# A four-layer graph kernel: smaller-edge masks of a quarter's own blocks move from VectorE to ScalarE, and one share step moves behind them

## The chip, the cores and the metric

The kernel runs on one core of a Trainium2 chip. The metric is the device time of the whole program in microseconds (us), lower being better. Profiles come from one execution each; times in a profile count from the start of its span. TensorE is written PE, VectorE DVE, ScalarE ACT, GpSimd POOL and the DMA-issuing engine SP.

## What is computed

4096 nodes carry 64 features each. A 4096 x 4096 adjacency (about 1.6% of entries are positive, the diagonal is full, the rest zero) is used by four layers, each followed by a residual sum and a normalization of each row:

```python
x = _layernorm(x + _L0_gnn_ref(x, adj, L0_gnn_weight))      # Chebyshev, three products with adj
x = _layernorm(x + _L1_gnn_ref(x, adj, adj, ...))           # two GRU cells and a signed attention
x = _layernorm(x + _L2_gnn_ref(x, adj, ...))                # last 100 neighbours with decay
x = _layernorm(x + _L3_gnn_ref(x, adj, ...))                # hyperbolic aggregation
```

The change is in the second layer, whose core is

```python
A = adj - diag(diag(adj))
node_support = concat([(A > 0) @ h, (A < 0) @ h])
h_plus, h_minus = (A > 0) @ hw, (A < 0) @ hw
e_plus, e_minus = leaky_relu(concat([h_plus, h_minus]) @ a), leaky_relu(concat([h_minus, h_plus]) @ a)
att = softmax(where(A > 0, e_plus, where(A < 0, e_minus, -9e15)))
edge_support = (att * A) @ hw
```

An attention score depends only on the row and the sign of the edge. So the kernel needs four sums over neighbours of each node: with the positive part of A, with the negative part, with the 0/1 mask of edges above zero and with the 0/1 mask of edges below zero. It forms all four, although this input has no edge below zero.

## The kernel before

The second layer works on four quarters of 1024 columns (`q`, 0 to 3). Each quarter streams all 4096 rows through a ring of three slots of SBUF as 16 pairs (`m`, 0 to 15) of row blocks, a pair being 128 partitions x 2048 float32. For each pair:

- ACT makes `negs` = relu(-edges) (L1684), then on even pairs `less` = sign(negs) (L1688), then the codes that the third layer reads (`make_codes1`, L1665), and issues the store of these codes.
- DVE takes two steps of a running count of edges (`extend_chain`, L2405), makes `more` = edges > 0 (L2411), on odd pairs `less` = edges < 0 (L2441), and turns the edges into max(edges, 0) in place (L2444, called the rectified edges here), which must wait for `negs`.
- PE multiplies the rectified edges and `negs` (`edge_products`, L1088 and L1089; called the edge block here) and the two masks (`mask_products`, L1104; the mask block). On even pairs the edge block comes first, on odd pairs the mask block.

In a quarter's **own pairs**, those with m // 4 == q, the columns and rows meet on the diagonal. There DVE does more: it reads the diagonal (L2423, L2427) and cuts it out of the edges (L2430), between and behind its two chain steps. Only then may ACT read the edges (it waits for `diag_cut`), and DVE make the masks. On the other pairs ACT need not wait for DVE.

Orders are written out by hand, and each engine runs its own in sequence; semaphores tie them. Three of these ties matter below. The second chain step of pair m waits until ACT has made the codes of pair m - 1 (`extend_chain`: `codes_made`), so its room can be written again. `negs` and the masks have room for two pairs, so making those of pair m waits until PE is through with pair m - 2 (`pair_used`). And `mask_products` waits for all masks of the pair before its first matmul.

Work of the quarter before is spread over the pairs of the present one: `score_gate` (DVE, after m = 3), `exps` (ACT, m = 4), `share_gate` (DVE, after m = 5: small steps and the copy L2304), `spread_shares` (PE, before the products of m = 7, L1017), `weigh_sums` (DVE, after m = 8, L2310), `hidden` (PE, m = 11 and 12; it needs `weigh_sums`), `read_hidden` (ACT), and from the third quarter on the transposes and products of the third layer (`turn_rows`, `copy_rows`, `supports`). In the last quarter ACT also makes the first decays of the third layer (L1651) at m = 14 and 15, and `new_state` (L1589) at m = 15.

Of the kernel before, what the change touches and what calls it, by code (L numbers as in the profile page):

```python
# [7 lines left out]
ALU = mybir.AluOpType  # L8
# [38 lines left out]
def adjacency_stack(nc, adjT, x, xT, cheb_w, gatWT, gat_a2, wieT, wheT, bie, bhe, winT, whnT, bin_, bhn,  # L47
# [5 lines left out]
    with ctx:  # L53
# [11 lines left out]
        with ExitStack() as under:  # L65
            under.enter_context(nc.sbuf_tensor("ring_low", [P, RING1, GB, QC], F32))
            less = under.enter_context(nc.sbuf_tensor("less", [P, 2, 2, QC], F32R))
# [245 lines left out]
        n = 0  # L313
        for quad, end in enumerate(quad_ends):
            late = quad >= len(quad_ends) - 2
            n = max(n, end + (2 if late else 3), LAST_AT + 4)
# [25 lines left out]
            return u if u and u.turned else None  # L342

        PAIRS = 2 * NS
        L2_TILES = [(Q, s) for part in ((1, 2, 3, 0), (4, 5), (6, 7)) for Q in (0, 1) for s in part]
        L2_TILES += [(Q, s) for Q in (2, 3) for s in range(NS)]

# [93 lines left out]
        less_made = sem("less_made")  # L441
        masks_made = sem("masks_made")
# [197 lines left out]
        def used1(T):  # L640

            return 2 + 2 * (T + 1)

        def later_after(chain, j):

# [204 lines left out]
        def _(pe):  # L850
# [241 lines left out]
            def mask_products(q, m, r):  # L1092

                pe.wait_ge(masks_made, q * PAIRS + m + 1)
                if m % 2 == 0:
                    pe.wait_ge(less_made, (q * PAIRS + m) // 2 + 1)
                for i in range(2):
                    start, stop = m == 0 and i == 0, m == PAIRS - 1 and i == 1
                    for t, masks in enumerate((more, less)):
                        if start and q:  # L1100
                            pe.wait_ge(sums_copied[0], 3 * q - 1 + t)
                        for h in range(2):
                            cols = slice(h * HALF, (h + 1) * HALF)
                            mm = nc.tensor.matmul(ps[:, 2 + 2 * t + h, :], parts[:, 2 * m + i, :],  # L1104
                                                  masks[:, m % 2, i, cols], start=start, stop=stop)
                return mm

            for q in range(NQ):
                for m in range(PAIRS):
                    s, pair = divmod(m, 2)  # L1110
                    r = slot1(q, s)
                    if q == 0 and m == 10:
                        pe.wait_ge(turn_read, turns0)
                        turn_row_sums(NB - CB, NB, 7, visits[-1])
                    if q and m == 0:
                        turn_h(q - 1)
                    if q and m == 2:
                        score(q - 1)
                    if q and m == 7:
                        spread_shares(q - 1)  # L1120
                    if q >= 2 and m == 9:
                        turn_rows(q - 2)
                    if q >= 2 and m == 10:
                        supports(q - 2)
                    if q == 0 and m % 4 == 0:
                        pe.wait_ge(rest_made[0][0], s // 2 + 1)
                    hides = q and m in (11, 12)
                    if hides:
                        hidden(q - 1, 2 * (m - 11))
                    if m % 2:  # L1130
                        mask_products(q, m, r)
                        if hides:
                            hidden(q - 1, 2 * (m - 11) + 1)
                        edge_products(q, m, r).then_inc(pair_used, 1)
                    else:
                        edge_products(q, m, r)
                        if hides:
                            hidden(q - 1, 2 * (m - 11) + 1)
                        mask_products(q, m, r).then_inc(pair_used, 1)
# [308 lines left out]
        def _(act):  # L1448
# [76 lines left out]
            for a in visits:  # L1525
# [4 lines left out]
                if a.t in COUNT_TURN_AT:  # L1530
                    m = COUNT_TURN_AT.index(a.t)
# [139 lines left out]
            for q in range(NQ):  # L1671
                for m in range(PAIRS):
                    s, pair = divmod(m, 2)
                    r = slot1(q, s)
                    if q == 0 and m == 7:
                        norm_act(act, NQ - 1)
                        act.preload_act_table_set("exp_and_others")
                    if q == 0 and m == 9:
                        split_act(act, NQ - 1)
                    act.wait_ge(loaded[r], loads(q, s))  # L1680
                    if s // 2 == q:
                        act.wait_ge(diag_cut, m + 1)
                    act.wait_ge(pair_used, q * PAIRS + m + 1)
                    nc.scalar.activation(negs[:, pair], ring[:, r, 2 * pair:2 * pair + 2, :], ACT.Relu,  # L1684
                                         scale=-1.0).then_inc(negs_made, 1)
                    if m % 2 == 0:
                        act.wait_ge(negs_made, q * PAIRS + m + 1)
                        nc.scalar.activation(less[:, pair], negs[:, pair], ACT.Sign).then_inc(less_made, 1)  # L1688
                    make_codes1(q, m)
                    if q and m == 0:  # L1690
                        copy_sums(q - 1)
                    if q and m == 1:
                        copy_h(q - 1)
                    if q and m == 4:
                        exps(q - 1)
                    if q >= 2 and m == 7:
                        root1(q - 2)
                    if q >= 2 and m == 9:
                        copy_rows(q - 2)
                    if q >= 2 and m == 10:  # L1700
                        read_supports(q - 2)
                        part2(q - 2, 0)
                    if q and m == 11:
                        read_hidden(q - 1, range(2))
                    if q and m == 12:
                        read_hidden(q - 1, range(2, 6))
                    if q and m == 13:
                        read_hidden(q - 1, range(6, CB))
                    if q >= 2 and m == 13:
                        part2(q - 2, 1)  # L1710
                    if q and m == 15:
                        new_state(q - 1)
                    if q >= 2 and m == 15:
                        part2(q - 2, 2)
                    if q == NQ - 1 and m in (14, 15):
                        make_decays(m - 14)
# [230 lines left out]
        def _(dve):  # L1947
            V = nc.vector
# [459 lines left out]
            def make_more(q, m, edges):  # L2408

                dve.wait_ge(pair_used, q * PAIRS + m + 1)  # L2410
                return V.tensor_scalar(more[:, m % 2], edges, 0.0, None, ALU.is_gt)  # L2411

            for q in range(NQ):
                for m in range(PAIRS):
# [3 lines left out]
                    edges = ring[:, r, 2 * pair:2 * pair + 2, :]  # L2418
                    if m == 0:
                        open_chain(q)  # L2420
                    if s // 2 == q:
                        mine = own_blocks(ring[:, r], s % 2, pair)
                        V.tensor_tensor(own, mine, ident[:].unsqueeze(1).broadcast_to([P, 2, P]),  # L2423
                                        ALU.mult).then_inc(diag_steps, 1)
                        extend_chain(q, 2 * m, edges[:, 0, HALF:QC])
                        dve.wait_ge(diag_steps, 2 * m + 1)
                        V.tensor_reduce(diag[:, 2 * m:2 * m + 2], own, AX_X, ALU.add).then_inc(diag_steps, 1)  # L2427
                        extend_chain(q, 2 * m + 1, edges[:, 1, HALF:QC])
                        dve.wait_ge(later_made, later_after(NQ + q, min(2 * m + 2, NB - 1)))
                        V.tensor_tensor(mine, mine, offdiag[:].unsqueeze(1).broadcast_to([P, 2, P]),  # L2430
                                        ALU.mult).then_inc(diag_cut, 1)
                        dve.wait_ge(diag_cut, m + 1)
                    else:
                        extend_chain(q, 2 * m, edges[:, 0, HALF:QC])
                        if m % 2:
                            make_more(q, m, edges)
                        extend_chain(q, 2 * m + 1, edges[:, 1, HALF:QC])
                    if m % 2:
                        if s // 2 == q:
                            make_more(q, m, edges)  # L2440
                        V.tensor_scalar(less[:, pair], edges, 0.0, None, ALU.is_lt).then_inc(masks_made, 1)  # L2441
                    dve.wait_ge(later_made, later_after(NQ + q, min(2 * m + 2, NB - 1)))
                    dve.wait_ge(negs_made, q * PAIRS + m + 1)
                    V.tensor_scalar(edges, edges, 0.0, None, ALU.max).then_inc(rect_ready, 1)  # L2444
# [26 lines left out]
                        score_gate(q - 1)  # L2471
                    if q >= 2 and m == 4:
                        centre_rows(1, q - 2)
                    if q and m == 5:
                        share_gate(q - 1)
                    if q >= 2 and m == 6:
                        row_spread(1, q - 2)
                    if q >= 2 and m == 7:
                        scale_rows1(q - 2)
                    if q and m == 8:  # L2480
                        weigh_sums(q - 1)
                    if m == PAIRS - 1:
                        cut_own_edges(q)
# [495 lines left out]
```

## Time and profile before

| | us |
|---|---|
| median of 3 runs | 1470.06 |
| lowest and highest run | 1464.03, 1471.13 |
| the profiled execution | 1466.39 |
| its span, first to last instruction | 1464.7 |
| second layer in its trace, about | 477 to 907 |

Over the span PE is busy 90%, DVE 82%, ACT 67%, POOL 15%. A busy PE is not one at its peak: the page models the ends of matmuls. The page has a row of the clock granted to TensorE; in this kernel it is 2.4 GHz nearly throughout, and falls to 1.2 GHz in short stretches. A timeline row gives the start, the duration, the engine, the line, the operands and their shape, and in brackets how long the engine was idle before and what released it. The difference to the metric (1.7 us here) lies outside the span.

### The profile page before, as it was taken

The numbers are of one execution on the slowest core, as the hardware profiler recorded it, in microseconds if no ns is written. First come the engines' busy times: TensorE is split into PE (matmuls) and PEld (weight loads), VectorE is DVE, ScalarE is ACT, GpSimd is POOL, SyncE is SP. The second block draws the span as 40 slices with busy tenths as digits, with TensorE's granted clock in tenths as the row PEclk, the third lists the DMA queues.
The fourth block names the chain that finished last, engine by engine and source line by source line (L and its number), as shares of the span: only waits on it lengthen the run. The fifth ranks groups of instructions, "written<-read, shape, count | busy, mean of one in ns | idle before, by whom it ended". The sixth has DMA issues, their size and how long they took to land. (4 is left out here: it accounts for less than half of the span.)

```text
span 1464.7 us, 18440 instructions
## 1 busy us (share of the span) xinstructions
PE 1322.8 (90%) x6874; PEld 589.6 (40%) x6874; DVE 1201.0 (82%) x1554; ACT 983.7 (67%) x919; POOL 222.6 (15%) x150
## 2 busy tenths in 40 slices
PE   6899999999898999999999999989978888888893
PEld 1233334334334444444544554544423433334342
DVE  5898978995887888867977977558688898899997
ACT  0001444894583677567677767786789899999985
POOL 1000000000000000000000001152133354444450
PEclk9999999999998999999999999999889999999995
DMA  9999979998999555544535532244534666546610
GB/s 360 409 409 409 372 263 413 409 391 325 415 409 413 199 200 197 191 150 173 194 134 190 191 136 103 75 150 147 203 114 126 202 172 216 193 153 222 218 50 29
DMA packets 134561, 341.56 MB, mean 233 GB/s; under 512 B 7877, under 2 KB 57481, under 8 KB 134281
## 3 DMA queue, kind: packets, MB, share of 16 engines
q1 hardware_dynamic: 118240, 320.88, 59.6%
q10 hardware_dynamic: 16232, 19.51, 3.9%
q8 instruction: 55, 0.90, 0.3%
q14 instruction: 34, 0.27, 0.1%
HBM read 321.49 MB, written 17.83 MB: 232 GB/s over the span
## 5 line engine op out<-in xcount | busy, mean ns | idle before, releaser
L1088 PE MATMUL ps<-ring,X 128*64 128x512 f32 x512 | 236.7, 611 | 11.8 <-DVE ring L2444 6.6
L1089 PE MATMUL ps<-work,X 128*64 128x512 f32 x512 | 236.8, 612 | 0.0
L844 POOL TENSOR_TENSOR ring<-ring,work 128x1024 f32<-128x1024 f32 x72 | 170.1, 2362 | 222.8 <-DVE work L2836 222.8
L1684 ACT ACTIVATE work<-ring 128x2048 f32<-128x2048 f32 x64 | 122.4, 1912 | 85.9 <-PE ps L1104 37.8
L821 POOL TENSOR_SCALAR work<-ring 128x1024 int16<-128x1024 uint8 x24 | 27.4, 1143 | 955.0 <-DMA ring<-codes 889.9
L951 PE MATMUL ps<-ring,work 128*64 128x512 f32 x704 | 160.0, 602 | 1.5 <-DVE Y L2102 1.5
L2444 DVE TENSOR_SCALAR ring<-ring 128x2048 f32<-128x2048 f32 x64 | 78.4, 1224 | 66.9 <-ACT work L1684 66.5
L1088 PEld LDWEIGHTS ps<-ring,X 128*64 128x64 f32 x512 | 67.5, 139 | 150.3 <-issue 140.1
L2124 DVE TENSOR_TENSOR work<-work,ring 128x1024 f32<-128x1024 f32 (+1 forms) x92 | 104.9, 1140 | 4.9 <-DMA ring<-in_adjT 3.1
L1433 ACT ACTIVATE turn_in<-ps 128x512 f32<-128x512 f32 x12 | 7.2, 596 | 144.9 <-PE ps L951 144.0
L1267 PE MATMUL ps<-work 64*128 64x512 f32 x288 | 88.0, 690 | 16.5 <-DVE work L2851 15.0
L1511 ACT ACTIVATE work<-ring 128x4096 bf16<-128x4096 f32 x23 | 83.0, 3615 | 29.2 <-PE ps L900 26.9
L1493 ACT ACTIVATE work<-work,code_bias 128x2048 uint8<-128x2048 bf16 (+1 forms) x32 | 62.2, 1944 | 59.0 <-DVE work L2163 45.3
L951 PE MATMUL ps<-ring,X 128*64 128x512 f32 x352 | 82.9, 614 | 12.4 <-DMA ring<-in_adjT 12.3
L1104 PE MATMUL ps<-more,parts 128*128 128x512 f32 x256 | 84.2, 410 | 4.9 <-DVE less L2441 4.8
L2851 DVE SCALAR_TENSOR_TENSOR work<-ps,work 128x1024 f32<-128x1024 f32 x72 | 87.5, 1215 | 1.1 <-PE ps L1278 1.1
L2405 DVE SCALAR_TENSOR_TENSOR stage_words<-ring,stage_words 128x512 bf16<-128x512 f32 x124 | 85.1, 686 | 3.6 <-DVE stage_words L2405 0.5
L951 PEld LDWEIGHTS ps<-ring,work 128*64 128x64 f32 x704 | 48.8, 138 | 97.0 <-issue 96.1
L2411 DVE TENSOR_SCALAR more<-ring 128x2048 fp32r<-128x2048 f32 x64 | 78.4, 1225 | 6.7 <-PE ps L1089 5.2
L1104 PE MATMUL ps<-less,parts 128*128 128x512 f32 x256 | 79.3, 391 | 0.0
L1836 ACT ACTIVATE work<-work 128x1024 f32<-128x1024 f32 x72 | 75.4, 1047 | 1.7 <-DVE work L2851 0.5
L1665 ACT ACTIVATE work<-stage_words,code_bias 128x1024 uint8<-128x1024 bf16 (+1 forms) x64 | 71.0, 1109 | 5.1 <-DVE stage_words L2405 5.0
(387 smaller groups left out, 2695.2 us busy)
## 6 DMA issues: line engine op xcount, KB each, us to landing
ring<-in_adjT SPq DMA_DIRECT2D x86, 2048.0 KB, 13.5
work<-in_adjT SPq DMA_DIRECT2D x26, 2048.0 KB, 23.1
ring<-in_adjT SPq DMA_DIRECT2D x24, 1024.0 KB, 8.8
ring<-in_adjT SPq DMA_DIRECT2D x48, 512.0 KB, 3.9
ring<-codes SPq DMA_DIRECT2D x32, 512.0 KB, 3.8
ring<-in_adjT SPq DMA_DIRECT2D x64, 256.0 KB, 3.3
codes<-work ACTq DMA_DIRECT2D x32, 256.0 KB, 6.2
codes<-work ACTq DMA_DIRECT2D x64, 128.0 KB, 2.4
```

The source lines that it names most:

```text
L844: nc.gpsimd.tensor_tensor(u.edges[:, cols], u.edges[:, cols], u.angle[:, cols], ALU.mult).then_inc(weighted, 1)
L951: mm = nc.tensor.matmul(ps[j * F:(j + 1) * F, TURN_BANKS[n] + h, :], (X, T1, T2)[p][:, a.g * GB + k, :], a.room[:, k, cols], start=start, ...
L1088: nc.tensor.matmul(ps[0:F, h, :], rows, ring[:, r, 2 * (m % 2) + i, cols], start=start, stop=stop)
L1089: mm = nc.tensor.matmul(ps[F:P, h, :], rows, negs[:, m % 2, i, cols], start=start, stop=stop)
L1104: mm = nc.tensor.matmul(ps[:, 2 + 2 * t + h, :], parts[:, 2 * m + i, :], masks[:, m % 2, i, cols], start=start, stop=stop)
L1267: mm = nc.tensor.matmul(ps[:, u.banks + h, :].rearrange("p (t c) -> p t c", t=2), UT[h * F:(h + 1) * F, b * P:(b + 1) * P], u.columns(node ...
L1511: nc.scalar.activation(signs[:, a.sign_half].rearrange("p k c -> p (k c)"), a.room.rearrange("p k c -> p (k c)"), ACT.Sign).then_inc(tile_ ...
L1684: nc.scalar.activation(negs[:, pair], ring[:, r, 2 * pair:2 * pair + 2, :], ACT.Relu, scale=-1.0).then_inc(negs_made, 1)
L2124: ins = V.tensor_tensor(sums, sums, edges, ALU.add)
L2405: V.scalar_tensor_tensor(later1[:, (j + 1) % GB, :], edges, 0.0, later1[:, j % GB, :], ALU.not_equal, ALU.add).then_inc(later_made, 1)
L2411: return V.tensor_scalar(more[:, m % 2], edges, 0.0, None, ALU.is_gt)
L2851: V.scalar_tensor_tensor(u.angle, ps[:, u.banks:u.banks + 2, :].rearrange("p h c -> p (h c)"), 0.5 * DIST_SCALE, u.angle, ALU.max, ALU.add ...
```

## The change

In every pair that holds own edges, ACT makes `less` on odd pairs too, from `negs` by sign. DVE's comparison is left out there, and its `more` carries the signal that the comparison carried. Two odd pairs of each quarter are concerned, eight in all. The other 24 odd pairs stay as they were.

In the second quarter (q = 1), whose own pairs are m = 4 to 7, `share_gate` moves from m = 5 to m = 7, `spread_shares` from 7 to 9 and `weigh_sums` from 8 to 10. In the third and fourth quarter they stay. No DMA is added, removed or moved.

```diff
+        SHARE_GATE_AT, SPREAD_SHARES_AT, WEIGH_SUMS_AT = (None, 7, 5, 5), (None, 9, 7, 7), (None, 10, 8, 8)
...
+        def cuts_own(q, m):
+
+            return m // 4 == q
+
+        def less_by_sign(q, m):
+
+            return m % 2 == 0 or cuts_own(q, m)
+
+        def signs_of_less(q, m):
+
+            return sum(less_by_sign(n // PAIRS, n % PAIRS) for n in range(q * PAIRS + m + 1))
...
                 pe.wait_ge(masks_made, q * PAIRS + m + 1)
-                if m % 2 == 0:
-                    pe.wait_ge(less_made, (q * PAIRS + m) // 2 + 1)
+                if less_by_sign(q, m):
+                    pe.wait_ge(less_made, signs_of_less(q, m))
...
-                    if q and m == 7:
+                    if q and m == SPREAD_SHARES_AT[q]:
                         spread_shares(q - 1)
...
-                    if m % 2 == 0:
+                    if less_by_sign(q, m):
                         act.wait_ge(negs_made, q * PAIRS + m + 1)
                         nc.scalar.activation(less[:, pair], negs[:, pair], ACT.Sign).then_inc(less_made, 1)
                     make_codes1(q, m)
...
                     if m % 2:
-                        if s // 2 == q:
-                            make_more(q, m, edges)
-                        V.tensor_scalar(less[:, pair], edges, 0.0, None, ALU.is_lt).then_inc(masks_made, 1)
+                        if cuts_own(q, m):
+                            make_more(q, m, edges).then_inc(masks_made, 1)
+                        else:
+                            V.tensor_scalar(less[:, pair], edges, 0.0, None, ALU.is_lt).then_inc(masks_made, 1)
...
-                    if q and m == 5:
+                    if q and m == SHARE_GATE_AT[q]:
                         share_gate(q - 1)
...
-                    if q and m == 8:
+                    if q and m == WEIGH_SUMS_AT[q]:
                         weigh_sums(q - 1)
```

## Rows read from the trace of the kernel before

**Rows 1.** The page: busy time, share of the span, instructions.

```profile
PE 1322.8 (90%) x6874; PEld 589.6 (40%) x6874; DVE 1201.0 (82%) x1554; ACT 983.7 (67%) x919; POOL 222.6 (15%) x150
```

**Rows 2.** Groups of instructions, 477 to 905 us: busy us, mean ns, idle before.

```profile
L1684 ACT ACTIVATE work<-ring 128x2048 f32<-128x2048 f32 x64 | 122.4, 1912 | 85.9 <-PE ps L1104 37.8 <-DVE ring L2430 28.9 <-PE ps L1089 10.9
...
L1088 PE MATMUL ps<-ring,X 128*64 128x512 f32 x508 | 235.0, 612 | 11.8 <-DVE ring L2444 6.6 <-DVE work L2249 5.2
...
L1104 PE MATMUL ps<-more,parts 128*128 128x512 f32 x256 | 84.2, 410 | 4.9 <-DVE less L2441 4.8
...
L2441 DVE TENSOR_SCALAR less<-ring 128x2048 fp32r<-128x2048 f32 x32 | 39.1, 1220 | 0.0
```

**Rows 3.** Timeline, first quarter, pairs 2 and 3: start, duration, engine.

```profile
489.81 1.91 ACT L1684 ACTIVATE work<-ring 128x2048 f32<-128x2048 f32 x1 [2.90 <-DVE ring L2430]
491.75 1.91 ACT L1688 ACTIVATE less<-work 128x2048 fp32r<-128x2048 f32 x1
493.57 1.13 ACT L1665 ACTIVATE work<-stage_words,code_bias 128x1024 uint8<-128x1024 bf16 x1
...
497.35 1.92 ACT L1684 ACTIVATE work<-ring 128x2048 f32<-128x2048 f32 x1 [2.65 <-DVE ring L2430]
...
499.72 0.73 PE L1104 MATMUL ps<-more,parts 128*128 128x512 f32 x2 [0.89 <-DVE less L2441]
```

**Rows 4.** Timeline, second quarter, pairs 5 to 7.

```profile
602.47 1.92 ACT L1684 ACTIVATE work<-ring 128x2048 f32<-128x2048 f32 x1 [1.33 <-issue]
...
604.84 0.73 PE L1104 MATMUL ps<-more,parts 128*128 128x512 f32 x2
...
610.40 1.91 ACT L1684 ACTIVATE work<-ring 128x2048 f32<-128x2048 f32 x1 [4.98 <-DVE ring L2430]
...
613.73 0.64 PE L1088 MATMUL ps<-ring,X 128*64 128x512 f32 x1 [3.20 <-DVE ring L2444]
...
619.01 0.72 PE L1104 MATMUL ps<-more,parts 128*128 128x512 f32 x2
...
620.96 1.95 PE L1017 MATMUL ps<-ident,work 128*128 128x128 f32 x16
622.66 0.70 PE L1104 MATMUL ps<-more,parts 128*128 128x512 f32 x2
```

**Rows 5.** Timeline, third quarter, pairs 9 to 11.

```profile
740.97 1.92 ACT L1684 ACTIVATE work<-ring 128x2048 f32<-128x2048 f32 x1 [3.18 <-DVE ring L2430]
...
743.33 0.73 PE L1104 MATMUL ps<-more,parts 128*128 128x512 f32 x2 [0.98 <-DVE less L2441]
...
745.60 0.68 DVE L2405 SCALAR_TENSOR_TENSOR stage_words<-ring,stage_words 128x512 bf16<-128x512 f32 x1
...
746.82 1.91 ACT L1684 ACTIVATE work<-ring 128x2048 f32<-128x2048 f32 x1 [1.27 <-issue]
...
753.76 1.92 ACT L1684 ACTIVATE work<-ring 128x2048 f32<-128x2048 f32 x1 [0.38 <-DVE ring L2430]
```

**Rows 6.** Timeline, fourth quarter, pair 15 and the end of the layer.

```profile
899.24 1.91 ACT L1684 ACTIVATE work<-ring 128x2048 f32<-128x2048 f32 x1 [1.77 <-DVE ring L2430]
...
901.61 0.73 PE L1104 MATMUL ps<-more,parts 128*128 128x512 f32 x2 [1.55 <-DVE less L2441]
...
907.35 0.60 ACT L1556 ACTIVATE work<-ps 128x512 f32<-128x512 f32 x1 [0.43 <-PE ps L1089]
```

**Rows 7.** Two more pauses of PE, then windows with the granted clock (PEclk).

```profile
393.81 0.38 PE L911 MATMUL ps<-early_w,turn_in 128*128 128x128 f32 x1 [2.84 <-ACT turn_in L1433]
...
685.88 0.82 PE L1088 MATMUL ps<-ring,X 128*64 128x512 f32 x1 [2.17 <-DVE work L2249]
...
393.80:398.00 4.20, 2.74 (x26) 2.12 (x28) 4.00 (x6) 3.46 (x1) 0.00 (x0) 1.00 1.03 416
613.70:617.10 3.40, 3.37 (x10) 1.07 (x12) 3.36 (x6) 1.59 (x2) 0.00 (x0) 0.61 1.02 401
901.60:905.00 3.40, 3.39 (x16) 1.92 (x18) 2.70 (x6) 3.00 (x4) 0.00 (x0) 1.00 0.12 41
```

More of the change, by code:

```diff
@@ L2420, in _ @@
                         open_chain(q)
-                    if s // 2 == q:
+                    if cuts_own(q, m):
                         mine = own_blocks(ring[:, r], s % 2, pair)
@@ L2438, in _ @@
                     if m % 2:
-                        if s // 2 == q:
-                            make_more(q, m, edges)
-                        V.tensor_scalar(less[:, pair], edges, 0.0, None, ALU.is_lt).then_inc(masks_made, 1)
+                        if cuts_own(q, m):
+                            make_more(q, m, edges).then_inc(masks_made, 1)
+                        else:
+                            V.tensor_scalar(less[:, pair], edges, 0.0, None, ALU.is_lt).then_inc(masks_made, 1)
                     dve.wait_ge(later_made, later_after(NQ + q, min(2 * m + 2, NB - 1)))
```

## The prediction

> **What bounds the kernel now.** By the page PE is the busiest engine, 90% of the span [rows 1], but a share over the span does not say what this change can touch, so I read the second layer alone, 477 to 907 us. Grouped there by line, PE's main groups show 11.8 us idle before edge blocks and 4.9 us before mask blocks [rows 2]: 16.7 us at most is to be had from removing waits, and only part of it lies in own pairs. The rest of the layer is PE-bound: outside own pairs ACT waits for PE (37.8 and 10.9 us before L1684), inside them for DVE's cut of the diagonal (28.9 us) [rows 2]. Then I read the timeline pair by pair. In own pairs the order is a ring: cut (DVE), `negs` (ACT), rectify (DVE), cut of the next pair. From `negs` to the next `negs` it takes 6.94 us behind an even pair (746.82 to 753.76) and 5.85 us behind an odd one (740.97 to 746.82) [rows 5], 12.8 us for two pairs. An edge block takes about 3.6 us of PE (235.0 us over 64 pairs, less a little overlap [rows 2]) and a mask block about 1.95 (619.01 to 620.96 [rows 4]). Two pairs are thus 11.1 us of PE: the own pairs are where PE overtakes the other two engines and pauses.
>
> The pauses in own pairs that the change can reach are: first quarter 0.89 us before the masks of pair 3 [rows 3]; second quarter 3.20 us before the edges of pair 6 [rows 4]; third quarter 0.98 us before the masks of pair 9 [rows 5]; fourth 1.55 us before the masks of pair 15 [rows 6]. The 3.20 costs more than itself: the clock granted behind it is 0.61 of full [rows 7], and the edge block of pair 6 takes from 613.73 to 619.01 [rows 4], 5.28 us where it takes 3.6 at 2.4 GHz, so 1.7 us more at 1.2 GHz.
>
> **What leaves DVE.** Eight comparisons of 1.22 us [rows 2], 9.8 us in sum. But what follows each on DVE, the rectifying, needs `negs`: it cannot start before about 2.0 us after `negs` does (1.91 us [rows 3] and the semaphore), and now it starts when the comparison ends, some 2.3 us after. So only 0.2 to 0.3 us of each 1.22 us comes forward. The rest becomes idle time of DVE.
>
> **What ACT takes on.** Eight signs of 1.91 us [rows 3], 15.3 us. Where they stand matters, not their sum. In an odd pair the comparison runs beside `negs`; the sign runs behind it. Call T the start of `negs`. Before, PE starts the masks at T + 2.37 (497.35 to 499.72 [rows 3]; 602.47 to 604.84 [rows 4]; 899.24 to 901.61 [rows 6]; 740.97 to 743.33 [rows 5]): four times the same. After, the sign ends at T + 3.85 (489.81 to 491.75 + 1.91 [rows 3]) and PE starts at T + 3.90. That is **1.53 us later in every odd own pair where PE is waiting already**, and PE is in order: the edge block and everything behind it wait with it.
>
> The sign also pushes the codes: they end at T + 4.89 (489.81 to 493.57 + 1.13 [rows 3]) instead of T + 2.95 (1.82 + 1.13 by the same spacing), and DVE's second chain step of the next pair waits for them. Before, that step starts at T + 4.63 (740.97 to 745.60 [rows 5]); without the comparison it could at T + 4.4; now it starts at T + 4.95. From it to the next `negs` it is 1.22 us (745.60 to 746.82 [rows 5]), so the next `negs` starts at T + 6.17 where it was T + 5.85. **The ring is 0.3 us longer, not shorter.** I assume that semaphores cost what they do in the same places now.
>
> Here the Trainium skill speaks against the change. "ScalarE: Activation LUTs", Rules for kernel authors, wants simple elementwise work on VectorE rather than ScalarE. This trace agrees for this shape, 1.91 against 1.22 us [rows 2, 3]. The page's figures of about 0.3 us and 0.83 ns for each element would make 2.0 us of a sign, an estimate, and the masks 0.1 us later still; the rows decide.
>
> **What the moved shares give** (second quarter only). Behind pair 5 the next `negs` comes at 7.93 us (602.47 to 610.40 [rows 4]) where 5.85 is usual: 2.08 us are `share_gate`. Moved behind pair 7 it lies beside 7 us of PE backlog, with no cut to be made for pair 8; `spread_shares` and `weigh_sums`, two pairs later, still come before `hidden` at m = 11. If that cover were missing, the 2.08 us would return. I cost it at nothing.
>
> **The sum, quarter by quarter**, following PE.
> - First: pair 1's codes delay pair 2 by 0.34 us, which pair 3 inherits; its masks start at 497.69 + 3.90 = 501.6 instead of 499.72. **+1.9 us.** The pause grows to 2.5 us.
> - Second: masks of pair 5 start at 606.37 instead of 604.84 (pause 1.8). `negs` of pair 6 start at 602.47 + 6.17 = 608.6 instead of 610.40, the rectified edges are ready 3.3 us later, at 611.9, just when PE ends the edges of pair 5 (608.4 + 3.6). The 3.20 us pause and its clock drop vanish: masks of pair 6 at 615.6 instead of 619.01. `negs` of pair 7 start at 615.6, its masks at 619.5 (pause 1.9) where they started at 622.66, but before them stood `spread_shares`, which is now still to be done and takes 1.65 us net (from 620.96 to 622.66, less the overlap). 619.5 - 622.66 + 1.65 = **-1.5 us.**
> - Third: masks of pair 9 at 744.87 instead of 743.33, **+1.5 us**, pause 2.5 us. What follows on ACT (copies for the third layer, then `negs` of pair 10, some 0.7 us later) hides in PE's delay.
> - Fourth: pair 13 has its masks due only after `hidden`, so nothing. Pair 15: 903.14 instead of 901.61, **+1.5 us**, pause 3.1 us. ACT's further work there, `new_state` and a decay, ends 1.9 us later than now, about when the last block does; ACT waited 0.43 us for PE there [rows 6], so at most 0.1 us is added.
>
> Together +3.4 us. The last pair ends the layer, and behind it PE starts the third layer at once (907 us), so I let it pass 1 to 1 into the end.
>
> **The clock.** The trace does not show pauses of 2.5 us in this place. PE fell to 1.2 GHz behind the 3.20 us pause (0.61) and ran slow too behind one of 2.17 us at 685.88, but not behind 2.84 us at 393.81 (1.00), nor behind 1.55 us at 901.61 (1.00) [rows 6, 7]. So each of the three pauses of 2.5, 2.5 and 3.1 us costs between nothing and 1.7 us; none for those of 1.8 and 1.9, at most 1.7 for one of them. I take two of three: **+3.4 us**. Bounds 0 and +6.8.
>
> Sum: +6.8 us. Against the profiled execution that is 1466.4 + 6.8 = 1473.2; that one lies 3.7 us below the median of the three runs, which themselves spread over 7 us. Against the median it gives 1476.9; I forecast between the two, nearer to the median: **1476.0 us**.
>
> **The rivals.**
> - *No clock drops* (the pauses stay without effect, as the one at 393.81): +3.4 us, 1473.5. Same mechanism; for it speaks the mixed record in rows 7.
> - *Every pause drops the clock*: 3.4 + 4 x 1.7 = +10.2 us, 1480.
> - *Faster: DVE is the bound of own pairs.* If the next cut did not wait for codes and sign (because the chain step found its semaphore already up, or ACT overlapped `negs` and sign), each odd own pair would shorten the ring by 1.2 us, the pauses of 0.89, 0.98 and 1.55 would go and with the 3.20 + 1.7 of pair 6 the gain would be 8.3 us: 1462. It decides from the point at which the masks are ready by T + 2.4; the sign is at T + 3.9, against it. A weaker form: PE has enough work in hand at pairs 3, 9 and 15 that the later masks are not noticed; then only pair 6 counts, -5 us, 1465. Against it: PE is already waiting at each of them.
>
> **How the numbers follow.** Forecast with two drops, or one or three at 1.7 us either side: 0.45. No drops: 0.23. All drops and ACT late besides: 0.17. Faster, either form: 0.15. One measurement of this kernel can tell about 0.5%, 7.35 us, from no change. The forecast lies just inside that, so its own chance divides: slower 0.20, same 0.25. No drops: same 0.20, slower 0.03. All drops: slower 0.15, same 0.02. Faster case: 0.08 beyond 0.5%, 0.07 inside. Sums: faster 0.08, same 0.54, slower 0.38. The range takes in the bounds of the clock (1473.5 to 1480), some 2 us of spread, and the weaker faster case: **1465.0 to 1482.0**.
>
> **What would show it.** Right: masks of odd own pairs start 3.9 us behind their `negs`; PE's idle time before L1104, 4.9 us now, grows to 11 or more, released by ACT; the pause before the edges of pair 6 is gone; `negs` to `negs` behind an odd own pair is 6.2 us. Wrong: PE's pauses before the masks of pairs 3, 9, 15 at 1.5 us or less, or PE waiting at m = 11 of the second quarter for `weigh_sums`.

## The result and the profile after

| | before | after |
|---|---|---|
| median of 18 runs, us | 1471.32 | 1476.63 |
| lowest and highest | 1464.03, 1478.66 | 1471.49, 1482.02 |
| the profiled execution | 1466.39 | 1474.91 |
| its span | 1464.7 | 1473.2 |

The ratio after to before is 1.0043, with a 95% interval from 1.0029 to 1.0058: slower by 6.3 us, between 4.3 and 8.5; the two medians lie 5.3 us apart. In the two profiled executions the difference is 8.5 us, and it stands at 8.5 when the third layer's first matmul starts (908.35 before, 916.86 after). Behind that point it swings between 7.8 and 12.7 us, with stretches of low clock that stand at different places in the two traces, and comes back to 8.5 at the end.

The part behind the second layer matters for reading every trace below. Its instructions are the same in all kernels of this document, and yet it takes from 557.4 us (before) to 567.5 us (e3) in the traces (557.6 in after), counted from PE's first work behind the last block of the second layer. So the second layer is also compared by itself, from the start of its first `negs` to that same point: 430.2 us before, 438.8 after.

The page after, engines, and the groups of the second layer (line L1684 of before is L1697 now, L1688 is L1701, L1088 is L1101, L1104 is L1117, L2441 is L2455):

```profile
PE 1320.3 (90%) x6874; PEld 586.3 (40%) x6874; DVE 1192.2 (81%) x1546; ACT 999.5 (68%) x927; POOL 224.0 (15%) x150
```

```profile
L1101 PE MATMUL ps<-ring,X 128*64 128x512 f32 x512 | 233.5, 604 | 10.6 <-DVE ring L2458 5.4 <-DVE work L2262 5.2
L1697 ACT ACTIVATE work<-ring 128x2048 f32<-128x2048 f32 x64 | 122.4, 1912 | 72.6 <-PE ps L1117 27.9 <-DVE ring L2443 23.9 <-PE ps L1102 13.4
L2458 DVE TENSOR_SCALAR ring<-ring 128x2048 f32<-128x2048 f32 x64 | 78.4, 1225 | 74.8 <-ACT work L1697 74.4
...
L1117 PE MATMUL ps<-more,parts 128*128 128x512 f32 x256 | 85.8, 417 | 15.7 <-ACT less L1701 12.7 <-DVE less L2455 3.0
...
L1701 ACT ACTIVATE less<-work 128x2048 fp32r<-128x2048 f32 x40 | 76.5, 1912 | 1.3
L2455 DVE TENSOR_SCALAR less<-ring 128x2048 fp32r<-128x2048 f32 x24 | 29.3, 1220 | 0.0
```

DVE has lost the eight comparisons of 1.22 us (29.3 us in L2455 where [rows 2] has 39.1) and ACT has gained eight signs. PE's idle time before the mask blocks has grown from 4.9 us [rows 2] to 15.7, and 12.7 us of it ends with a sign on ACT, a releaser that [rows 2] does not have.

The timeline of PE at the masks of pairs 3 (first quarter), 5 and 7 (second), 9 (third) and 15 (fourth), with the idle time before each:

```profile
501.50 0.47 PE L1117 MATMUL ps<-more,parts 128*128 128x512 f32 x1 [2.52 <-ACT less L1701]
608.33 0.47 PE L1117 MATMUL ps<-more,parts 128*128 128x512 f32 x1 [1.70 <-ACT less L1701]
621.43 0.47 PE L1117 MATMUL ps<-more,parts 128*128 128x512 f32 x1 [1.93 <-ACT less L1701]
747.18 0.47 PE L1117 MATMUL ps<-more,parts 128*128 128x512 f32 x1 [2.62 <-ACT less L1701]
907.32 0.77 PE L1117 MATMUL ps<-more,parts 128*128 128x512 f32 x1 [3.46 <-ACT less L1701]
```

They answer to 499.72, 604.84, 622.66, 743.33 and 901.61 [rows 3 to 6]. The timeline of ACT in the second quarter shows why:

```profile
604.33 1.92 ACT L1697 ACTIVATE work<-ring 128x2048 f32<-128x2048 f32 x1 [1.33 <-issue]
606.27 1.91 ACT L1701 ACTIVATE less<-work 128x2048 fp32r<-128x2048 f32 x1
608.09 1.13 ACT L1678 ACTIVATE work<-stage_words,code_bias 128x1024 uint8<-128x1024 bf16 x1
...
610.49 1.91 ACT L1697 ACTIVATE work<-ring 128x2048 f32<-128x2048 f32 x1 [1.27 <-DVE ring L2443]
```

The masks of pair 5 start 4.00 us behind the start of `negs` (604.33 to 608.33) where it was 2.37, and the next `negs` come 6.16 us behind (610.49) where it was 7.93 with the share step between [rows 4]. The edge block of pair 6 starts at 613.82 without a pause.

The windows behind four of these pauses, then (their eighth column is the granted clock):

```profile
501.50:504.90 3.40, 3.40 (x16) 1.94 (x18) 0.73 (x2) 2.91 (x3) 0.00 (x0) 1.00 0.12 41
621.40:624.80 3.40, 3.37 (x12) 1.87 (x14) 2.54 (x7) 2.91 (x3) 0.00 (x0) 0.72 0.17 60
...
747.20:750.60 3.40, 3.40 (x16) 1.94 (x18) 1.61 (x4) 2.96 (x6) 0.00 (x0) 1.00 0.11 39
907.30:914.00 6.70, 6.68 (x18) 3.54 (x20) 2.45 (x2) 5.23 (x4) 0.00 (x0) 0.57 0.06 20
```

The pauses of 2.52 and 2.62 us left the clock at 2.4 GHz; one of 1.93 brought 1.2 GHz soon behind it, and the one of 3.46 brought it for nearly 7 us.

How far the kernel after lies behind the one before, read at the same block of PE in both traces:

| at | us behind | what came in between |
|---|---|---|
| last pair of the first quarter | 1.86 | masks of pair 3, 1.8 |
| last pair of the second | 2.21 | +0.35 |
| last pair of the third | 3.80 | masks of pair 9, 1.6 |
| masks of pair 15 of the fourth | 5.71 | +1.9 |
| first matmul of the third layer | 8.51 | clock at 1.2 GHz, 2.65; a longer wait ahead of it, 0.15 |

When the layer starts, the kernel after stands 0.2 us ahead (first `negs` at 476.84 against 477.02), so the first quarter itself costs 2.0 us.

### The profile page after: what moved, and what is told of

Read it like the earlier page. It is cut to its first block and busy times, and to the rows that moved or that the text cites. A ratio compares the mean times of both kernels' runs of the same rounds, so it can differ in the third digit from the quotient of the medians.

```text
span 1473.2 us, 18448 instructions
## 1 busy us (share of the span) xinstructions
PE 1320.3 (90%) x6874; PEld 586.3 (40%) x6874; DVE 1192.2 (81%) x1546; ACT 999.5 (68%) x927; POOL 224.0 (15%) x150
## 5 line engine op out<-in xcount | busy, mean ns | idle before, releaser
L1101 PE MATMUL ps<-ring,X 128*64 128x512 f32 x512 | 233.5, 604 | 10.6 <-DVE ring L2458 5.4
L1102 PE MATMUL ps<-work,X 128*64 128x512 f32 x512 | 233.6, 605 | 0.0
L1697 ACT ACTIVATE work<-ring 128x2048 f32<-128x2048 f32 x64 | 122.4, 1912 | 72.6 <-PE ps L1117 27.9
L2458 DVE TENSOR_SCALAR ring<-ring 128x2048 f32<-128x2048 f32 x64 | 78.4, 1225 | 74.8 <-ACT work L1697 74.4
L1101 PEld LDWEIGHTS ps<-ring,X 128*64 128x64 f32 x512 | 66.9, 139 | 147.6 <-issue 139.6
L1524 ACT ACTIVATE work<-ring 128x4096 bf16<-128x4096 f32 x23 | 83.0, 3615 | 29.3 <-PE ps L913 27.1
L1117 PE MATMUL ps<-more,parts 128*128 128x512 f32 x256 | 85.8, 417 | 15.7 <-ACT less L1701 12.7
L964 PE MATMUL ps<-ring,X 128*64 128x512 f32 x352 | 82.1, 609 | 12.4 <-DMA ring<-in_adjT 12.3
L1117 PE MATMUL ps<-less,parts 128*128 128x512 f32 x256 | 80.7, 397 | 0.0
L1701 ACT ACTIVATE less<-work 128x2048 fp32r<-128x2048 f32 x40 | 76.5, 1912 | 1.3
```

The costliest lines, as they stand in the source:

```text
L964: mm = nc.tensor.matmul(ps[j * F:(j + 1) * F, TURN_BANKS[n] + h, :], (X, T1, T2)[p][:, a.g * GB + k, :], a.room[:, k, cols], start=start, ...
L1101: nc.tensor.matmul(ps[0:F, h, :], rows, ring[:, r, 2 * (m % 2) + i, cols], start=start, stop=stop)
L1102: mm = nc.tensor.matmul(ps[F:P, h, :], rows, negs[:, m % 2, i, cols], start=start, stop=stop)
L1524: nc.scalar.activation(signs[:, a.sign_half].rearrange("p k c -> p (k c)"), a.room.rearrange("p k c -> p (k c)"), ACT.Sign).then_inc(tile_ ...
```

## The experiments

Theory A is that of the prediction: in an odd own pair the sign runs behind `negs` instead of beside it, PE stands waiting for exactly that mask, and the moved shares are a gain of their own. (The last part turns out to hold for the kernel before only.) The main rival, B, is that VectorE is the bound in own pairs, so its relief must help there. Times below are medians, ratios are to the kernel before on the same chip with 95% intervals; positions in a trace come from one profiled execution each.

**e1 and e2: the two parts apart.** e1 is the kernel before with one edit, e2 the changed kernel with the opposite one:

```diff
+        SHARE_GATE_AT, SPREAD_SHARES_AT, WEIGH_SUMS_AT = (None, 7, 5, 5), (None, 9, 7, 7), (None, 10, 8, 8)   # e1
...
+        SHARE_GATE_AT, SPREAD_SHARES_AT, WEIGH_SUMS_AT = (None, 5, 5, 5), (None, 7, 7, 7), (None, 8, 8, 8)    # e2
```

Expected of e1:

> The kernel before with only the moved share steps of the second quarter; the smaller-edge masks of own odd pairs stay on VectorE. Theory A (the sign, run behind negs, makes masks late; the moved shares are a pure gain): negs of pair 6 start 5.85 us behind those of pair 5 instead of 7.93, the 3.20 us pause before its edge block shrinks to about 1.2 us, the clock stays at 2.4 GHz there, and the layer ends 3.4 us earlier than before, all of it in the second quarter; ratio about 0.9977. Rival B (the relief of VectorE by the signs is what the move needs, without it the move gains nothing or costs): 0 or up to +2 us, a new pause at pairs 8 to 11.

Expected of e2:

> The changed kernel with the share steps back at their old places. Theory A: +1.9 us in the first quarter, +0.3 us in the second (negs of pair 6 8.25 us behind those of pair 5 where 7.93 were), +1.5 each in the third and fourth, so +5.2 us, plus 0 to 1.7 us for each of the three pauses of 2.5 to 3.5 us that may drop the clock: ratio 1.0035 to 1.007. Rival B (VectorE was the bound of own pairs): each odd own pair comes up to 1.2 us earlier, ratio 0.997 or less.

e1 takes 1468.57 us, ratio 0.9986 (0.9973 to 1.0000), a gain of about 2 us by an interval that just reaches no change; e2 1478.01 us, 1.0046 (1.0023 to 1.0069), a loss of about 7. The two parts pull in opposite directions, and the signs are the larger. Their second layers alone take 427.3 and 440.0 us, where 430.2 stood before. In e1's trace, ACT and then PE:

```profile
603.23 1.92 ACT L1685 ACTIVATE work<-ring 128x2048 f32<-128x2048 f32 x1 [1.32 <-issue]
...
609.08 1.91 ACT L1685 ACTIVATE work<-ring 128x2048 f32<-128x2048 f32 x1 [2.90 <-DVE ring L2431]
```

```profile
612.40 0.64 PE L1089 MATMUL ps<-ring,X 128*64 128x512 f32 x1 [1.11 <-DVE ring L2445]
```

`negs` to `negs` is 5.85 us, as expected, and the pause of 3.20 us [rows 4] has become 1.11, without low clock. Over the second quarter e1 wins 2.8 us in its trace (3.4 expected), and less than 0.1 in each of the others. In e2 the masks of pairs 1, 3, 5, 7, 9 and 15 start 4.00 or 4.01 us behind `negs`, every one; pairs 3, 9 and 15 pause 2.50, 2.59 and 3.46 us. Here, unlike in the trace of after, the clock did fall behind pair 3 and pair 9: the same pauses, another outcome. B, which asked for a ratio of 0.997 or less, is out.

The second quarter of e2 did not go as expected. It was to lose 0.3 us and wins 1.5: `negs` of pair 6 come 7.73 us behind those of pair 5 (8.25 expected, 7.93 before), because `share_gate` covers the later codes, and PE, itself later at pair 5, finds a shorter pause at pair 6, 1.38 us instead of 3.20, behind which the clock stays up:

```profile
617.51 0.64 PE L1101 MATMUL ps<-ring,X 128*64 128x512 f32 x1 [1.38 <-DVE ring L2458]
```

So signs and moved shares both remove the one pause before pair 6, and it can be removed only once. Alone each wins in the second quarter, 1.5 and 2.8 us; together, in the trace of after, they lose 0.35, or win 1.3 without the slow stretch behind pair 7. On top of the signs the moved shares thus give nothing that these runs show: ratio 1.0046 without them, 1.0043 with them.

**e3: codes ahead of the sign.** The changed kernel, but in odd own pairs ACT makes and stores the codes first. It tells apart the two ways in which a sign can hurt: through its mask, or through the codes for which VectorE's chain waits.

```diff
+                    if m % 2 and cuts_own(q, m):
+                        make_codes1(q, m)
                     if less_by_sign(q, m):
                         act.wait_ge(negs_made, q * PAIRS + m + 1)
                         nc.scalar.activation(less[:, pair], negs[:, pair], ACT.Sign).then_inc(less_made, 1)
-                    make_codes1(q, m)
+                    if not (m % 2 and cuts_own(q, m)):
+                        make_codes1(q, m)
```

> The changed kernel, but in odd own pairs ScalarE makes and stores the codes before the sign. Theory A1 (what costs is that PE waits for the sign): masks start at T + 5.0 instead of T + 3.9 (T is the start of negs), the ring is 0.5 us shorter; against the changed kernel +0.6 us in the first and second quarter, +1.1 in the third and fourth, +3.4 us in all. Theory A2 (what costs is that the codes hold up VectorE's chain of the next pair): the next negs come 5.66 us instead of 6.17 us behind and the kernel is 1 to 2 us faster than the changed one.

It takes 1486.86 us, ratio 1.0116 (1.0088 to 1.0145), from four runs: against the changed kernel 10 to 11 us slower, where A1 said +3.4 and A2 a gain. Its trace, ACT and PE at pair 3:

```profile
497.72 1.91 ACT L1697 ACTIVATE work<-ring 128x2048 f32<-128x2048 f32 x1 [2.64 <-DVE ring L2446]
499.54 1.13 ACT L1678 ACTIVATE work<-stage_words,code_bias 128x1024 uint8<-128x1024 bf16 x1
500.70 0.33 ACTq L1681 DMA_DIRECT2D codes<-work  x1
501.07 1.91 ACT L1703 ACTIVATE less<-work 128x2048 fp32r<-128x2048 f32 x1 [0.40 <-ACT work L1678]
```

```profile
503.12 0.47 PE L1117 MATMUL ps<-more,parts 128*128 128x512 f32 x1 [2.06 <-ACT less L1703]
```

The next `negs` of the second quarter did come 5.66 us behind, as A2's mechanism has it, and it helped nothing; the mask at T + 5.4 decides (T is the start of `negs`). I had forgotten the issue of the store, 0.33 us on ACT's own queue and 0.40 before the next ACTIVATE, so it was 5.4 and not 5.0. Pair 1, which pauses 0.48 us in the trace of after, now pauses 1.59 us. The pauses before the masks of pairs 5, 9 and 15 were 3.1, 4.0 and 4.9 us, each with 1.2 GHz behind it, and the mean granted clock of its four runs is 0.955 against 0.961 in 18 runs of the changed kernel. The traces tell where the rest lies. The second layer takes 443.0 us in e3 and 438.8 in after: 4.3 us more, close to the 3.4 of A1, though made up otherwise (+0.8, -0.7, +3.1 and +1.2 us by quarter where +0.6, +0.6, +1.1 and +1.1 were expected; the third has a slow stretch more). Of the 14.9 us between the two traces, 9.9 lie behind the second layer, where the instructions are the same, at a granted clock of 0.94 against 0.96; 0.7 lie ahead of it. So e3 loses about 4 us in the layer that it changes, and why all four of its runs (1483.3 and above) are slower than any of the changed kernel (1482.0 and below) is not shown.

**e4: the edge block first in odd own pairs.** The changed kernel with one condition more in PE's order:

```diff
-                    if m % 2:
+                    if m % 2 and not cuts_own(q, m):
                         mask_products(q, m, r)
```

> The changed kernel, but in odd own pairs PE multiplies the edge block before the mask block. Theory A1 (lateness of the sign, seen by PE because the masks stand first): PE starts at T + 3.3 with the edges instead of at T + 3.9 with the masks, 0.6 us earlier in each of the four quarters, so -2.4 us against the changed kernel, and its pauses before pairs 3, 9 and 15 are about 1.9, 1.9 and 2.5 us. Rival A2 (the ring of cut, negs, rectify, codes sets the time, PE's order does not matter): no difference to the changed kernel.

1474.57 us, ratio 1.0025 (1.0008 to 1.0042), some 2.6 us better than the changed kernel by the two ratios; 2.4 was expected. In the traces its second layer is 4.6 us shorter than that of after (434.2 against 438.8). Its pauses before pairs 3, 9 and 15 are 1.83, 1.91 and 2.51 us, released by VectorE's rectifying and no more by ACT:

```profile
500.97 0.64 PE L1101 MATMUL ps<-ring,X 128*64 128x512 f32 x1 [1.83 <-DVE ring L2458]
...
620.90 0.64 PE L1101 MATMUL ps<-ring,X 128*64 128x512 f32 x1 [1.23 <-DVE ring L2458]
...
744.48 0.64 PE L1101 MATMUL ps<-ring,X 128*64 128x512 f32 x1 [1.91 <-DVE ring L2458]
```

In the third quarter it gains 0.5 us, close to the forecast 0.6. In the first it gains nothing: PE starts pair 4 0.35 us earlier by its own order, but ACT's `negs` of pairs 4 and 8 start when they did, and by pair 8 both kernels stand alike. In the second it gains 2.1 us, of which 1.6 are a slow stretch that no longer follows pair 7 (its pause is 1.23 us at 620.90, where after has 1.93), and in the fourth 1.9, of which 1.2 are the clock's. Without the clock the four quarters give about 0, 0.5, 0.5 and 0.7 us, some 1.8 where 2.4 was expected; that the median came out so near was in part luck. PE's order matters, which speaks against A2, but only where ACT is not behind as well.

**e5, e6 and e6 again: shorten the ring itself.** If own pairs are bound by the ring, then VectorE's work should be put where it waits for `negs`. On even own pairs `more` is made ahead of rectifying, in the 2.1 us of waiting, and the sum of the diagonal's blocks moves behind the masks. No sign moves. e6 adds the moved shares.

```diff
                         V.tensor_tensor(own, mine, ident[:].unsqueeze(1).broadcast_to([P, 2, P]),
                                         ALU.mult).then_inc(diag_steps, 1)
                         extend_chain(q, 2 * m, edges[:, 0, HALF:QC])
-                        dve.wait_ge(diag_steps, 2 * m + 1)
-                        V.tensor_reduce(diag[:, 2 * m:2 * m + 2], own, AX_X, ALU.add).then_inc(diag_steps, 1)
...
                         dve.wait_ge(diag_cut, m + 1)
+                        if m % 2 == 0:
+                            make_more(q, m, edges).then_inc(masks_made, 1)
+                            sum_own(m)
...
-                    if m % 2 == 0:
+                    if m % 2 == 0 and s // 2 != q:
                         dve.wait_ge(rect_ready, q * PAIRS + m + 1)
                         make_more(q, m, edges).then_inc(masks_made, 1)
```

> The kernel before, but in even own pairs VectorE makes more before it rectifies, in the 2.1 us in which it waits for negs, and the sum of the diagonal's blocks stands behind the masks instead of between the chain steps. No sign is moved. Theory A (own pairs are bound by the ring cut, negs, rectify, next cut; what shortens that ring helps): negs behind an even own pair come after about 5.4 us instead of 6.94; the pauses of 0.89 (pair 3), 0.98 (pair 9) and 1.55 us (pair 15) vanish, the one of 3.20 us before pair 6 shrinks to about 1.5 us without a drop of the clock; -6 to -7 us against the kernel before, ratio 0.9955. Rival (ScalarE or PE is the bound there): within 1 us of the kernel before.

> The same with the moved share steps of the second quarter. Theory A: the pause before pair 6 goes too, about -9 us against the kernel before (ratio 0.994). If the two overlap in the second quarter only: -7 us.

> The kernel e6 once more, beside the two above on the same chip: 6 to 9 us faster than the kernel before, ratio 0.994 to 0.996.

e5: 1463.05 us, 0.9950 (0.9928 to 0.9971). e6: 1462.55 us, 0.9939 (0.9915 to 0.9962), and once more 1461.94 us, 0.9948 (0.9932 to 0.9963). This is 7.5 to 9 us faster than before and 14 faster than the changed kernel. Their second layers take 425.1 and 422.2 us (422.1 once more). In both, no pause over 0.2 us is left before the masks of pairs 3, 5, 7, 9 or 15. Two moves stand in this edit, `more` and the sum; which of them gives how much was not run apart. The second quarter was misjudged in e5: before pair 6 a pause of 2.87 us remained (1.5 expected), with the low clock behind; only with the shares moved does it shrink to 0.80. ACT in e6:

```profile
600.61 1.92 ACT L1685 ACTIVATE work<-ring 128x2048 f32<-128x2048 f32 x1 [0.55 <-issue]
...
606.66 1.91 ACT L1685 ACTIVATE work<-ring 128x2048 f32<-128x2048 f32 x1 [3.09 <-DVE ring L2435]
...
612.83 1.92 ACT L1685 ACTIVATE work<-ring 128x2048 f32<-128x2048 f32 x1 [1.27 <-DVE ring L2435]
```

and the groups of its second layer, where PE's idle time before masks is 2.4 us (4.9 in [rows 2], 15.7 after):

```profile
L1089 PE MATMUL ps<-ring,X 128*64 128x512 f32 x512 | 233.5, 604 | 9.5 <-DVE work L2250 5.2 <-DVE ring L2454 4.2
...
L1105 PE MATMUL ps<-more,parts 128*128 128x512 f32 x256 | 84.2, 410 | 2.4 <-DVE less L2449 2.4
```

Behind an even own pair the next `negs` now come 6.17 us behind (606.66 to 612.83) instead of 6.94, not 5.4 as I had said: with VectorE ahead, its second chain step has to wait for the codes, which on an even pair stand behind a sign anyhow. So 6.17 is what a sign in front of the codes leaves, on even pairs as on odd. (Pairs 8 and 10 of the third quarter, with more work on both engines, have 6.65 and 6.46.)

**e9: the change's signs on top of e6.** Would they have paid if VectorE's order had been better?

> The kernel of moved shares and more before rectifying (e6), with the change's signs in odd own pairs on top. In e6 the masks start 4.4 us behind negs in pair 1, 3.0 in pairs 3 and 5, 2.7 in 7, 2.6 in 9, 2.4 in 15. Theory A (a sign costs 3.9 us less this lag, wherever PE is waiting): +0.9 us at pair 3, +1.4 over the second quarter, +1.3 at pair 9, +1.5 at pair 15, nothing at pairs 1, 11 and 13: +5 us against e6, ratio to the kernel before 0.997 to 0.998. Rival (the signs would have paid if VectorE's order had been better): equal to e6 or faster.

1466.45 us, 0.9981 (0.9962 to 1.0001): 4 to 5 us slower than e6 once more, on the same chip; 5 expected. At pairs 1 and 13 nothing is lost (PE lags 4.4 and 7.6 us behind `negs` there), at pair 3 1.2 us, at pair 9 1.5; by the last pair of the third quarter it is 3.9 us behind e6 once more (3.6 expected):

```profile
740.85 0.47 PE L1117 MATMUL ps<-more,parts 128*128 128x512 f32 x1 [1.22 <-ACT less L1701]
```

**e7 and e8: signs in other places.** The kernel before, and e6, with signs in 11 odd pairs outside own pairs, where VectorE has no idle time and PE lags:

```diff
+        ACT_LESS = {(1, 1), (1, 15), (2, 1), (2, 3), (2, 5), (2, 7), (2, 15), (3, 1), (3, 3), (3, 5), (3, 7)}
...
+            return m % 2 == 0 or (q, m) in ACT_LESS
```

> The kernel before, with the sign on ScalarE in 11 odd pairs that hold no own edges and where VectorE runs without idle time: pairs 1 and 15 of the second quarter, 1, 3, 5, 7 and 15 of the third, 1, 3, 5, 7 of the fourth. Theory A (a sign costs only where PE is waiting for that mask and the next cut for the codes; where VectorE is the bound and PE lags behind negs by 4 us or more it gives 1.22 us each): pauses of PE before the first edge blocks of the third and fourth quarter shrink from 2.17 and 2.77 us to about 1 and 1.6 us, that before pair 8 of the third (1.03) vanishes, that at pair 1 of the second (1.41) shrinks to 0.3; -3 to -8 us, ratio 0.9945 to 0.998. Rival (a sign is dearer than the comparison wherever it stands, 1.91 against 1.22 us): slower by 0 to 5 us.

> Moved shares, more before the rectifying in even own pairs, and the 11 signs outside own pairs together. If the gains are of separate places they add up: -12 to -17 us against the kernel before, ratio 0.989 to 0.992. If PE's queue is full by then: no more than the better of the two.

Both missed. e7: 1469.42 us, 0.9986 (0.9971 to 1.0002). e8: 1463.01 us, 0.9943 (0.9921 to 0.9964), no better than e6 alone, though its trace is 0.7 us shorter. The trace of e7 shows VectorE at the seam of the second and third quarter:

```profile
679.20 1.23 DVE L2338 TENSOR_TENSOR work<-X,work 128x1024 f32<-128x1024 f32 x1 [1.66 <-ACT work L1599]
...
686.11 0.68 DVE L2259 COPY work<-ps 128x512 f32<-128x512 f32 x1
```

The sign of pair 15 stands ahead of `new_state` (L1599) on ACT, for which VectorE waits 1.66 us, and the copy for which PE waits comes later: the pause before the first edges of the third quarter grew from 2.17 [rows 7] to 2.78 us. At pair 1 of the second quarter PE did win 1.1 us, and had lost them again by pair 5, whose cut is due when it was before. The whole second layer of e7 takes 430.1 us, as before.

**e10: the copy that PE waits for, one place earlier.** e6, with the copy of the first sums ahead of `more` on VectorE at pair 0:

```diff
                     V.tensor_scalar(edges, edges, 0.0, None, ALU.max).then_inc(rect_ready, 1)
+                    if q and m == 0:
+                        copy_sums(q - 1)
```

Only the copy itself moves; the additions that followed it in `copy_sums` stay at their old place.

> e6 with the copy of the first sums, for which the first edge block of a quarter waits, before more instead of behind it on VectorE at pair 0. Theory G (VectorE has no idle time from the end of one quarter to pair 8 of the next, so what PE gains at pair 0 is given back by pair 8): the pauses of 2.2 and 2.7 us at pair 0 of the third and fourth quarter shrink by 1.2 us each, and at pair 9 both kernels stand where they stood: -0.5 us or less. Rival (the pause is a loss of its own): -2.4 us, and up to 3.4 us more where the clock no longer falls.

1460.52 us, 0.9933 (0.9908 to 0.9957), from four runs. By the medians that is 1.4 us less than e6 once more, on the same chip (0.9932 to 0.9963), which is too little to tell the -0.5 of G from the -2.4 of the rival; the traces have to. The pauses shrink as said, from 2.16 to 0.90 us at the third quarter and from 2.75 to 1.47 at the fourth, but a new one stands at pair 1:

```profile
679.57 0.61 PE L1089 MATMUL ps<-ring,X 128*64 128x512 f32 x1 [0.90 <-DVE work L2250]
...
686.59 0.50 PE L1105 MATMUL ps<-more,parts 128*128 128x512 f32 x1 [1.32 <-DVE less L2452]
```

At the end of the second quarter PE is 0.14 us ahead of the first e6, at pair 0 of the third 1.41, at pair 1 0.28, at pair 9 0.32. VectorE runs there without idle time, and what PE gains is taken back. In e6 once more PE also ran at 1.2 GHz at this pair 0, so e10 was 2.9 us ahead at its masks, and 0.1 at pair 9. A gain of PE ahead of such a stretch was no gain at its end.

## Why the prediction was right, point by point

- **Direction and size.** 1476.0 was forecast, 1476.63 measured, inside 1465 to 1482. That the two agree to 0.6 us is in part luck. The sum was +6.8 us, and 1476.0 lies between two starting points for it; the median of before, 1470.06 from three runs, is 1471.32 from 18. The profiled traces differ by 8.5, the second layers by 8.5, of which 4.3 without the clock (3.4 forecast) and 4.3 with it (3.4). The likeliest case, two drops of the clock, is also what the trace has, but only one of them, at pair 15, at a pause that I had named; the other came at pair 7.
- **The comparisons leave VectorE idle rather than faster.** Right: VectorE's idle time before rectifying rose to 74.8 us, most of it waiting for `negs`, from 66.9.
- **Masks 1.53 us later.** Right in kind, a little short: 1.63. They start at T + 4.00, not 3.90, in every odd own pair where PE waits. From the end of a sign on ACT to PE it takes 0.15 us here (606.27 + 1.91 to 608.33), where I had carried over the 0.05 of a comparison on VectorE.
- **The ring is 0.3 us longer.** Right: 6.17 against 5.85 (third quarter 6.45, where copies for the third layer follow on ACT). It costs 0.3 us in the first quarter, where `negs` of pair 3 start that much later counted from the layer's start, and nothing where `share_gate` covers it (e2). e3 shortened the ring to 5.66 and gained nothing by it, as its masks were later still; the ring was not tested by itself.
- **First quarter +1.9:** 1.86 measured, 2.0 from the layer's start. **Third +1.5:** 1.59. **Fourth +1.5:** 1.91; of the rest, 0.1 is the semaphore and 0.28 a later start of `negs` of pair 15, whose cause I did not find; e2 has the same 0.28.
- **Second quarter -1.5:** wrong in sign, +0.35. The masks of pair 6 came 1.61 us earlier where 3.4 less the 1.9 carried along is 1.5, the pause before the edges of pair 6 is gone, masks of pair 7 stand at 621.43. But behind that pause of 1.93 us PE ran at 1.2 GHz, which cost 1.6 us (7.12 us for the two blocks of pair 7 instead of 5.50) and which this line of the sum had at nothing. Without it the quarter gives -1.3.
- **The clock, +3.4.** 4.3 us in the trace, and wrong in its parts: nothing at pairs 3 and 9, 1.6 us at pair 7, 2.65 us at pair 15, where I had at most 1.7. In e2 it fell at pairs 3 and 9 as well, behind the same pauses, so a forecast of single drops could only hit by luck. By the ratio, 6.3 us less the 4.3 us that the quarters show without it leaves 2.0 us, between 0 and 4.2: how much the clock costs in a typical run is not shown.
- **The moved shares.** Right that they cost nothing: the cover held, and nothing waits for `weigh_sums` at pair 11. They gain on the kernel before (e1), but not on top of the signs (e2), since the signs alone already shorten the pause before pair 6 to 1.38 us. The prediction did not see this; it gave one figure for both parts.
- **Rival "VectorE is the bound of own pairs".** It fell with e2, which is slower. But its half-truth is e6: VectorE's order was a bound there, only not through the comparison.

## What to carry to other kernels

Before moving an operation to a less busy engine, write down when its result is ready in both places, counted from a common start, and compare that with the moment at which the consumer asks. Here ACT was idle enough for eight signs of 1.9 us, but each was ready 1.6 us later than the comparison that it replaced, behind its own input, and cost that much wherever PE was already waiting and nothing where PE lagged by 4 us or more. What helped instead was to fill the wait that an engine had in front of it anyway, 2.1 us of VectorE on even pairs, with work that it had been doing behind that wait, and to take a sum out of the way to the cut. Two parts of a change that shorten the same pause do not add up. And where a kernel's clock varies, compare the stage that was changed by itself: the untouched layers differed by up to 10 us between traces here.

## What the runs showed of the hardware

- A pause of PE does not decide by its length alone whether the clock falls. In the trace of after it stayed at 2.4 GHz behind 2.52 us (pair 3) and 2.62 us (pair 9). In e2, at the same two places, it fell to 1.2 GHz behind 2.50 and 2.59 us, and in after behind only 1.93 us (pair 7). The Trainium skill, "TensorE: Matmul & The Clock Gate", says under Part 1 that the change to the fast clock at a kernel's start varies from run to run, because the monitor does not start with the kernel. It does not say this of later falls; the two pairs of places here would fit it.
- The spread of one kernel's runs goes with its mean granted clock. In 29, 30 and 17 runs of the kernel before, on three chips, the two are correlated at -0.74, -0.55 and -0.68, some 8, 7 and 5 us for each 0.01 of clock. The mean clock of after's 18 runs, 0.9605, is no lower than the 0.9591, 0.9601 and 0.9599 of those, so the loss of the change does not show in the mean clock.
- Low clock did not always cost anything at the end. In the trace of before PE runs at 1.2 GHz behind the pauses before pair 0 of the third and fourth quarter, in that of after it does not. After is 1.7 us better off at the masks of pair 0 (0.51 us behind instead of 2.20), and 2.21 behind again at pair 6, because VectorE sets the pace there.
